# A GNN block on one core: row scales made tile by tile, a last block that leaves in five parts, and unread products from the first constant on

## What is computed

```
h  = relu(layernorm(x))                        # by row
xn = batchnorm(h)                              # by feature, over the 1250 rows
conv = relu((A xn / deg) @ W_conv + b_conv)    # A: the edge counts, 1250 x 1250
attn = random-feature attention of the first 256 rows of h, 8 heads
x  = x + batchnorm(conv + attn + h)            # end of layer 0
h  = relu(layernorm(x))
y  = ((1 + eps) h + A h) @ W1 + b1
y  = relu(batchnorm(y)) @ W2 + b2
out = x + h + relu(batchnorm(y))
```

## Time and profile before

| | before |
|---|---|
| median of 3 runs | 385.55 us (384.25 to 387.21) |
| the profiled execution | 384.12 us, its span 382.3 us |
| PE busy | 359.1 us, 94% of the span |
| DVE, ACT, POOL busy | 237.7, 174.1, 95.4 us |
| PE idle before its first matmul | 7.66 us |
| chain that ended last | PE 71%, DVE 11%, issue 7%, ACT 5%, POOL 4% |

### The profile page before, as it was taken

One profiled execution on the slowest core, in us unless ns is written; L12 is line 12 of the kernel. 1 busy time (PEld: TensorE's weight loads), 2 busy tenths in 40 slices (PEclk: granted clock), 3 DMA queues, 4 the chain that ended last, 5 costly groups with the idle time before them and its releaser, 6 DMA issues.

```text
span 382.3 us, 6046 instructions
## 1 busy us (share of the span) xinstructions
PE 359.1 (94%) x2027; PEld 275.4 (72%) x2027; DVE 237.7 (62%) x640; ACT 174.1 (46%) x302; POOL 95.4 (25%) x149
## 2 busy tenths in 40 slices
PE   1899998999999999999989997999999999999994
PEld 1577665767767657676556664559999999999992
DVE  5879699886877886627978887212354444532223
ACT  1437555778587136120076875212644543513121
POOL 7111003000000000000134879620557471201100
PEclk9999999999999999999999999999999999999998
DMA  6971300000000000004900032100000003020223
GB/s 188 293 189 74 111 4 1 4 1 3 3 3 3 3 3 3 3 2 118 245 19 1 2 110 79 36 0 2 0 2 1 0 11 101 0 55 13 69 54 80
DMA packets 16584, 18.03 MB, mean 47 GB/s; under 512 B 1813, under 2 KB 10965, under 8 KB 16537
## 3 DMA queue, kind: packets, MB, share of 16 engines
q1 hardware_dynamic: 15779, 17.28, 16.2%
q10 hardware_dynamic: 758, 0.16, 0.2%
HBM read 14.88 MB, written 2.56 MB: 46 GB/s over the span
## 4 chain that ended last, share of the span: by engine, by line
PE 71%; DVE 11%; issue 7%; ACT 5%; POOL 4%; DVEq 1%; DMA 1%; SPq 0%; POOLq 0%; ACTq 0%
PE bank L1280 68%; DVE hl L1168 1%; ACT hn L650 1%; POOL ln_s L457 1%; DVE w_lo L1187 1%; DVE st L988 1%; POOL x L498 1%; PE bank L1301 1%; DVE st_row L1179 1%; DVE ring L910 1%; PE bank L1654 1%; PE bank L1479 1%; DVE x L1176 1%; ACT hh L752 1%; DVE st_row L858 1%
## 5 line engine op out<-in xcount | busy, mean ns | idle before, releaser
L1280 PE MATMUL bank<-AT,hh 125*128 125x400 f16 (+1 forms) x240 | 80.9, 339 | 2.6 <-DVE hl L1168 2.6
L1280 PE MATMUL bank<-AT,hl 125*128 125x400 f16 (+1 forms) x240 | 80.7, 338 | 0.4 <-issue 0.4
L466 POOL TENSOR_TENSOR bn_tmp<-var_eps,minus_half 128x1 f32<-128x1 f32 (+1 forms) x15 | 10.3, 686 | 184.2 <-DVE var_eps L1002 184.1
L910 DVE TENSOR_SCALAR ring<-iota_code,code 125x250 f16<-125x250 f16 x200 | 46.1, 304 | 1.9 <-issue 1.8
L1280 PEld LDWEIGHTS bank<-AT,hh 125*128 125x128 f16 x240 | 23.2, 97 | 21.6 <-DVE hl L1168 3.2
L1280 PEld LDWEIGHTS bank<-AT,hl 125*128 125x128 f16 x240 | 23.4, 97 | 18.7 <-issue 0.9
L1280 PE MATMUL bank<-a_hi,w_hi 128*128 128x400 f32 (+1 forms) x96 | 34.2, 356 | 0.0
L1280 PE MATMUL bank<-agg_hi,w_hi 128*128 128x400 f32 (+1 forms) x96 | 34.0, 355 | 0.0
L1280 PE MATMUL bank<-a_hi,w_lo 128*128 128x400 f32 (+1 forms) x96 | 33.8, 352 | 0.0
L1280 PE MATMUL bank<-agg_hi,w_lo 128*128 128x400 f32 (+1 forms) x96 | 33.8, 352 | 0.0
L1280 PE MATMUL bank<-agg_lo,w_hi 128*128 128x400 f32 (+1 forms) x96 | 33.8, 352 | 0.0
(11 more groups left out here) (213 smaller groups left out, 744.8 us busy)
## 6 DMA issues: line engine op xcount, KB each, us to landing
x_in<-x SPq DMA_DIRECT2D x5, 448.0 KB
x<-x SPq DMA_DIRECT2D x2, 1120.0 KB
w_s<-w SPq DMA_DIRECT2D x2, 1024.0 KB, 9.8
w_s<-w SPq DMA_DIRECT2D x4, 512.0 KB, 3.8
out<-x SPq DMA_DIRECT2D x8, 224.0 KB
wB<-wk SPq DMA_DIRECT2D x1, 1024.0 KB, 7.9
wA<-wq SPq DMA_DIRECT2D x1, 1024.0 KB, 12.1
wC<-w_conv SPq DMA_DIRECT2D x1, 1024.0 KB, 15.6
```

The lines of the kernel that those rows point to most:

```text
L466: own.step(pool.tensor_tensor(bn_tmp[:, 1, k:k + n], var_eps[:, k:k + n], minus_half[:, 0:n], ALU.pow))
L910: return dve.tensor_scalar(ring[:, slot, j, a:b], iota_code[0:CH, a:b], code[:, bass.ds(c + j, 1)], float(-CODES * t), ALU.subtract, ALU.i ...
L1280: return pe.matmul(o, l, r, start=start, stop=stop, skip_group_check=True)
```

## The change

**Row scales.** DVE signals `s_mv` after every tile, POOL makes each tile's scale by itself, ACT waits for its own tile. DVE measures rows 0, 1, 2 before it reads the codes, rows 3 and 4 behind the first one-hot tiles, then `window_rows`, then row 5. ACT's start is interleaved: rows 0, 1, copy 0, row 2, copies 1 and 2, `K0`, row 3, `K1`.

**Unread products.** `ones16` is made by POOL's first instruction with a semaphore of its own, and PE starts 16 unread products (450 columns, fp16) as soon as it is there; 4 more follow the ranges, and 2, 2 and 4 follow `hT0`, `hT1` and `hT2`.

**Slots.** `RG` stands between `K0` and `K1`; `hT9` moves from slot 4 to slot 3; `FR` goes from ahead of `P UQ0` to behind them; in slot 11 `G3 R2` come before `MX1`, in slot 16 `G8` comes before `MX2 R7`; `SPLIT_AT` (when DVE makes `wC_lo`) goes from 7 to 6.

**The end.** The last block goes in five parts of two row tiles, in the order 1, 0, 3, 2, 4, parts 1 and 3 scaled by DVE. Its statistics are taken from PSUM before ACT evicts (ACT waits for `s_end_stats`), and `b2` is added to the mean afterwards. The last add of block 2 moves from between the statistics to behind the first term of the scales. Rows 0 to 111 of each part are stored by SP, rows 112 to 124 by ACT. 12 unread products instead of 20 stand before the last transposes.

```diff
 SLOTS:
-    "hT0 hT1 hT2 RG K0 K1", "hT3 hT4 PT Q0", "hT5 hT6 N1 Q1", "hT7 hT8 N0 UK0", "hT9 FR P UQ0", "V0", "MX0 V1", "QT0",
-    "G0 UK1", "KV0 UQ1 R0 G1", "O0 R1 G2", "MX1 R2 G3", ...
-    "MX2 R7 G8", ...
+    "hT0 hT1 hT2 K0 RG K1", "hT3 hT4 PT Q0", "hT5 hT6 N1 Q1", "hT7 hT8 hT9 N0 UK0", "P UQ0 FR", "V0", "MX0 V1", "QT0",
+    "G0 UK1", "KV0 UQ1 R0 G1", "O0 R1 G2", "G3 R2 MX1", ...
+    "G8 MX2 R7", ...
-SQ_AT, SPLIT_AT, H_AT = 2, 7, 6
+SQ_AT, SPLIT_AT, H_AT = 2, 6, 6
+SPARE = {"start": 16, "ranges": 4, "hT0": 2, "hT1": 2, "hT2": 4}
+END_TILES = [(0, 2), (2, 4), (4, 6), (6, 8), (8, 10)]
+END_ORDER, END_BANKS, END_DVE = (1, 0, 3, 2, 4), (7, 0, 1, 2, 6), (1, 3)
 POOL:
+            pool.memset(ones16[:], 1.0).then_inc(sem("s_ones"), 1)
-            for pair in range(T // 2):
-                pool.wait_ge(sem("s_mv"), pair + 1)
-                row_scales(2 * pair, 2, sem("s_rs"))
+            for i in range(T):
+                pool.wait_ge(sem("s_mv"), i + 1)
+                row_scales(i, 1, sem("s_rs"))
 ACT:
-            for i in range(3):
-                rows(i)
-            for i in range(3):
-                rows_T(i)
-            rows(3)
-            attention("K0")
+            rows(0)
+            rows(1)
+            rows_T(0)
+            rows(2)
+            rows_T(1)
+            rows_T(2)
+            attention("K0")
+            rows(3)
 ACT, u_out:
+                if f == FB - 1:
+                    act.wait_ge(sem("s_end_stats"), ci + 1)
 ACT, at the end:
+            for n, j in enumerate(END_ORDER):
+                act.wait_ge(sem("s_out"), 3 * (FB - 1) + n + 1)
+                store(act, FB - 1, j, ROWS[1])
 DVE:
-            for i in range(4):
+            for i in range(3):
                 row_stats(i)
...
+            row_stats(3)
             row_stats(4)
+            window_rows()
             row_stats(5)
-            window_rows()
...
+                        ps = read_group(dve, f"U{f}{ci}")[:, 0:w]
+                        feature_stats(f, ci, ps).then_inc(sem("s_end_stats"), 1)
...
+                    own.step(dve.tensor_scalar(mv_f[:, f, 0:1], mv_f[:, f, 0:1], pcol("b2", f), None, ALU.add))
+                    last_scales(..., lambda: out_add(f - 1, (2,)))
 PE:
+            pe.wait_ge(sem("s_ones"), 1)
+            keep_busy(SPARE["start"], banks[0])
             pe.wait_ge(sem("s_const"), NCONST)
...
                 for name in SLOTS[t]:
                     attention(name)
+                    keep_busy(SPARE.get(name, 0), banks[0])
...
-            keep_busy(20, open_group(pe, "spare"))
-            out_rows(FB - 1, range(3))
+            keep_busy(12, open_group(pe, f"out{FB - 1}3"))
+            out_rows(FB - 1, END_ORDER)
```

More of the change, by code:

```diff
@@ L144, in plan_banks @@
             n += 1
-        for j in range(3):
+        for j in range(len(OUT_TILES) if f < FB - 1 else 0):
             take(f"out{f}{j}", 6 + (3 * f + j) % 2)
-    take("spare", 0)
+    for j, bank in enumerate(END_BANKS):
+        take(f"out{FB - 1}{j}", bank)
     return place
-PLACE = plan_banks()
 W1_AT = (3, 7)
@@ L366, in load_x, with store @@
                    .then_inc(sem(f"d_x{pair}"), 16)
-        NCONST = 16
+        def store(eng, f, j, r):
+            t0, t1 = out_tiles(f)[j]
+            eng.dma_start(out_t[r, t0:t1, f * P:(f + 1) * P], x1[r, t0:t1, f * P:(f + 1) * P])\
+               .then_inc(sem("d_out"), 16)
+        NCONST = 15
         block = ctx.enter_context(nc.Block())
@@ L410, in _ @@
             for f in range(FB):
[L411 to L416, removed]
+                for n, j in enumerate(out_order(f)):
+                    sp.wait_ge(sem("s_out"), 3 * f + n + 1)
+                    for r in ROWS if f < FB - 1 else ROWS[:1]:
+                        store(sp, f, j, r)
+            sp.wait_ge(sem("d_out"), 16 * len(ROWS) * sum(len(out_tiles(f)) for f in range(FB)))
         @block.gpsimd
@@ L1149, in _, with last_scales @@
                 piece(name)
-            def last_scales(k, g, b, root, done):
+            def last_scales(k, g, b, root, done, meanwhile=lambda: None):
                 own.mark(dve.scalar_tensor_tensor(bn_tmp[:, 0, k:k + 1], mv_f[:, k, 0:1], -1.0, g, ALU.mult, ALU.mult))
+                meanwhile()
                 dve.wait_ge(root, 1)
@@ L1249, in out_add @@
                     u = ps[0:L, 0:(t1 - t0) * P].rearrange("p (t d) -> p t d", d=P)
-                    own.step(dve.scalar_tensor_tensor(o, u, 0.0, o, ALU.max, ALU.add))
+                    ins = dve.scalar_tensor_tensor(o, u, 0.0, o, ALU.max, ALU.add)
+                    if f == FB - 1:
+                        ins.then_inc(sem("s_out"), 1)
+                        continue
+                    own.step(ins)
                     dve.sem_inc(free[PLACE[f"out{f}{j}"][0]], 1)
@@ L1269, in _ @@
                     w2_low(3)
-            f, (t0, t1) = FB - 1, OUT_TILES[1]
+            f = FB - 1
             dve.wait_ge(full[PLACE[f"out{f - 2}2"][0]], PLACE[f"out{f - 2}2"][1] + 1)
-            dve.tensor_scalar(orr[:, f % 2, t0 * L:t1 * L], ur[:, f % 2, t0 * L:t1 * L], bn_s[:, f:f + 1],
-                              bn_t[:, f:f + 1], ALU.mult, ALU.add).then_inc(sem("s_o1"), 1)
-            out_add(f, range(3))
+            for ci in range(NC):
+                bank, turn = PLACE[f"U{f}{ci}"]
+                dve.wait_ge(free[bank], turn + 1)
+            for j in END_DVE:
+                t0, t1 = END_TILES[j]
+                dve.tensor_scalar(orr[:, f % 2, t0 * L:t1 * L], ur[:, f % 2, t0 * L:t1 * L], bn_s[:, f:f + 1],
+                                  bn_t[:, f:f + 1], ALU.mult, ALU.add).then_inc(sem(f"s_e{j}"), 1)
+            out_add(f, END_ORDER)
         @block.tensor
@@ L1280, in mm, with keep_busy @@
                 return pe.matmul(o, l, r, start=start, stop=stop, skip_group_check=True)
+            def keep_busy(n, ps):
+                for _ in range(n):
+                    mm(ps[:, 0:COLS[0][1]], ones16[:], ones16[:, 0:1].broadcast_to([P, COLS[0][1]]), True, True)
+            pe.wait_ge(sem("s_ones"), 1)
+            keep_busy(SPARE["start"], banks[0])
             pe.wait_ge(sem("s_const"), NCONST)
@@ L1296, in _ @@
             close_group(ins, "ranges")
+            keep_busy(SPARE["ranges"], banks[0])
             def turn_rows(i, rows, slots, h_done, name):
```

48 lines of the change are left out of this document (30 added, 18 removed), and 4 rows, old and new, of the table SLOTS.

## The result

| | before | after |
|---|---|---|
| median | 384.99 us of 4 runs (384.25 to 387.21) | 389.76 us of 4 runs (388.96 to 390.52) |
| the profiled execution, its span | 384.12, 382.3 us | 388.96, 387.2 us |
| PE busy | 359.1 us | 365.6 us |

The change made the kernel **slower by 1.1%**: the ratio is 1.0114, with the interval 1.0062 to 1.0165. The forecast was 383.2 us, with a range from 379.3 to 386.8.

What follows compares the result with a forecast made beforehand. PE, busy 94% of the span, bounds the kernel; its waits at the start, slots and last block were targeted. 0.5 + 1.8 = 2.3 us less gives 381.8, or 383.2 us as median; range 379.3 to 386.8.

Steps and rivals of the forecast that it cites:

- The end: Last block: earlier statistics, two-tile parts and split stores save 1.8 us, with bounds of 1.3 and 2.25.
- Step (b): Slot 3: hT9 must wait for ACT to copy hT7 out of bank 7, so PE stands 2.1 us.
- Step (c): Before V1: DVE's extra work delays the exponentials and V0's copy; V1 starts at 56.4, PE 0.8 us late.
- Step (d): Ahead of G0: batch norm terms come about 5 us earlier, so the 1.21 us wait goes; lead 0.5.
- Step (e): Slot 11: G3 R2 ahead of MX1 cover the only wait for attn, 0.6 us; lead 1.1.
- Step (f): Slot 16: with G8 first, PE waits for hn_lo with MX2 and R7 still to do; 0.6 us lost.
- K0's products at the high clock: Start: unread products bring PE to 2.4 GHz, so K0 and K1 take 7.1 us, 2.3 us less.
- The start: Up to window 0: sooner rows and faster key products put the first window at 21.4 us, PE leading by 4.2.
- step (a): Window 1's tiles: DVE and ACT hardly start earlier, PE waits 1.3 us ahead of hT5; lead falls to 2.9.
- The base: Starting time: the profiled execution lay 1.4 us under the median of 385.55, so 381.8 became 383.2 us.
- the rivals: Alternative outcomes: moves cost nothing (chance 0.27, 379.3), clock stays low (0.12, 386 to 387.3), end gives nothing (0.11, 385.0).
- the clock stays low: Rival, chance 0.12: pauses between rows return PE to 1.2 GHz, K0 starts near 17; 386 to 387.3 us.

Runs made afterwards that it cites:

- E2: The kernel before with only the last block's edits, including 12 unread products there; 382.41 us, ratio 0.9953.
- E3: The changed kernel with slots 3 and 4 and SPLIT_AT as in the kernel before; 384.48 us, ratio 0.9913 over its four lowest runs.
- E7: E3 with slot 16 also as in the kernel before (MX2 R7 G8); 383.65 us, ratio 0.9983.
- E8: The changed kernel with the load of w2 block 1 held back to layer 1's first big product; 390.61 us, ratio 1.0157.
- E12: The changed kernel with the loads of w2 blocks 0 and 1 both held back; 387.39 us, ratio 1.0025 over five of eight runs.
- E4: The changed kernel without the skipped block of 120 products and its branch; 385.37 us, ratio 1.0015.
- E9: The changed kernel without the 16 unread products at the start; 385.16 us, ratio 1.003.
- E1: The kernel before with 28 unread one-column products added behind PE's wait for the constants; 389.2 us, ratio 1.0122.
- E5: E3 with only the 16 unread products at the start kept, the 12 later ones removed; 381.66 us, ratio 0.9921.

## Why the prediction was wrong

**Right, by its own steps.** The end: 1.8 forecast; 1.9 in after and, counted from the last product, in E2. Step (b): 2.1 us forecast, 2.10 measured. Step (c), the start of `V1`: 56.4 forecast, 56.65. Step (d): no wait ahead of `G0`. Step (e): no wait for `attn` among PE's. Step (f): 0.6 us forecast, 0.7 between E3 and E7. K0's products at the high clock.

**The end, in part luck.** Its 1.8 was the middle of 1.3 and 2.25, from two prices of an ACT store, 0.65 and 0.45. The store cost 0.41, and ACT's queue didn't set the end: SP's last store was issued by 385.12, 0.4 us behind ACT's. The last add came 1.75 us nearer to the last product instead of 2.0 (5.53 us behind it, 7.28 before). That the middle fits is these two together.

**Off in size.** The start gave 3.15 us of 4.2: the clock fell at 9.5 us and the products ahead of K0 ran slowly, so K0 came at 15.15. This differs from run to run: of kernels whose first 40 us hold the same PE work, E8 and E12 had K0 at 14.10 and window 0 at 21.48, almost the forecast, and E4 had K0 at 16.65. The shortfall cost little further on. Behind step (a) the forecast had a lead of 2.9 us, 4.2 less a wait of 1.3 ahead of `hT5`; in after that wait didn't arise and the lead was 3.15. In E8 `hT5` waited 0.65 us; both met the same 2.1 us wait, and behind it E8 was ahead by 0.16 us of its 1.05. A later start does cost: E9 had K0 1.25 us behind after's and began layer 1 1.24 us behind it. The Trainium skill ("TensorE: Matmul & The Clock Gate", What's actually happening) says that the number of slow products at a start changes from run to run of one kernel. These traces agree, with K0 between 14.10 and 16.65.

The base was off too. The sum adds 1.4 us for the distance of the profiled execution from the median of three; over 9 to 26 more executions each time, the kernel before has medians of 384.1 to 384.5, which leaves 0.0 to 0.4.

**Wrong, step (c): 1.8 us.** It counted the wait ahead of `V1`, 2 to 3 us, and stopped there. But behind 2.76 us of idleness the clock was granted at 0.50 for 3.4 us, and PE, late already, had nowhere to win that back. The prediction had asked this of the start only, and had its answer from pauses of 1.2 us. So at 200 us PE was 1.25 us late instead of 0.5 early.

**Wrong, the term that was missing: 5.5 us.** The unread products were costed at nothing since "before 7.66 us PE has nothing to do". That is true of their time and not of their place in PE's list. The row that could have warned was the 1.32 us wait in front of row tile 9: an instruction behind a taken branch, with 0.45 us of "issue" idleness 14 products on. What the runs showed in place of nothing is a pause of 4.99 us there. The prediction names no wait of PE between 112 us and the last block, and takes everything there as unchanged. The pause (3.7 us) and the clock behind it (1.8) are more than the whole difference of the two kernels; E1, with the longer list alone, is 1.2% slower.

With both corrected the same sum gives 382.3 - 2.3 + 1.8 + 5.5 = 387.3 us for the span; 387.2 was measured. (That it agrees to a tenth is chance.)

None of the rivals was this. The one called "the clock stays low" gave the time nearest to the result, up to 387.3, but its condition, K0 behind 15.5, didn't come about.

**Open.** Why PE has 14 products at hand behind the branch with 0 and with 12 added, 12 with 16 and none with 28 (a plain count would fall evenly), and why some executions of the longer kernels seem to escape (one of ten in E1, two of ten in E3, perhaps two of eight in E12). The instructions' addresses are in no trace here.

## What to carry to other kernels

Work that costs no time can still cost a place: before adding instructions to an engine's list, look for a taken branch further down it, read the "issue" idleness just behind that branch, and time the list lengthened by empty instructions alone (E1 needed four lines). When a move makes a new wait on the matrix engine, add to the wait what the clock does behind it, from a row with a wait of that length. Test the parts of a mixed change singly: here one part was worth 0.5%, another cost 4.2 us, and the sum hid both.

## What the hardware showed that was not expected

- Waits of PE up to 1.8 us (E5, ahead of `G8`) were followed by no fall of the clock in the slots; each of 2.75 or 2.76 us by 3.4 us at 0.50 (after, E4, E8, E9, E12). The wait of 2.10 us was followed by one in E4, E8 and E12 and by none in after and E9. Windows of E8 behind its waits of 2.1 and 2.76 us:
```profile
41.40:44.70 3.30, 3.30 (x8) 0.80 (x6) 0.91 (x5) 0.58 (x1) 0.00 (x0) 0.50 0.00 0
58.50:61.80 3.30, 3.30 (x5) 1.34 (x4) 3.02 (x11) 1.51 (x5) 0.00 (x0) 0.50 0.00 0
```
- A one-column product takes 32 ns in a row of 28 (E1, 0.91 us for all).
- The clock column reads 1.00 before the first recorded change, even where products run at the low level: the earlier trace rows beside the earlier trace rows.
- Stores issued by ACT took 0.41 us each, no dearer than SP's 0.45.
